# A recommendation tower on one core: layer 2 turned round, layer 3 as a row sum on VectorE, and layer 1 of two sample tiles joined

## What is computed

```python
e = stack([tbl_f[ids[:, f]] for f in range(27)], axis=1)      # 512 x 27 x 128
z = einsum('bnd,bmd->bnm', e, e)[:, c, r]                      # 351 pairs per sample
h = concatenate([z, dense_ctx], axis=1)                        # 512 x 367
h = maximum(h @ W_top1 + b_top1, 0.0)                          # 512 x 512
h = maximum(h @ W_top2 + b_top2, 0.0)                          # 512 x 256
y = h @ W_top3                                                 # 512 x 1
```

## Time and profile before

| | us |
|---|---|
| median of 3 runs | 124.17 |
| lowest, highest run | 122.57, 124.36 |
| span of the profiled execution | 123.6 |
| TensorE matmul busy in it | 106.3 (86%) |
| VectorE busy | 70.0 (57%) |
| ScalarE busy | 67.2 (54%) |

### The profile page before, as it was taken

The page is one execution under the profiler, slowest core; times in us unless marked ns, Lnnn a source line. Parts: engine busy times, 40 slices in busy tenths (PEclk is TensorE's granted clock), DMA queues, the critical chain, the costliest instruction groups (busy, mean ns, idle before and its releaser), DMA issues.

```text
span 123.6 us, 3473 instructions
## 1 busy us (share of the span) xinstructions
PE 106.3 (86%) x1496; PEld 86.1 (70%) x1496; DVE 70.0 (57%) x98; ACT 67.2 (54%) x112; POOL 68.1 (55%) x71
## 2 busy tenths in 40 slices
PE   6998799899999899999329993789458999997992
PEld 6534487687887687788219883669448999797891
DVE  6799999999999999999900050015001060103401
ACT  4596929899999999995200052025301144531442
POOL 3777888888888888887744166416560665000000
PEclk9999999999999999999985599558975699999999
DMA  3896366966984574711210101110200011000000
GB/s 79 262 237 190 101 204 146 293 198 155 302 235 111 172 229 108 205 48 42 54 52 17 31 29 42 27 48 21 66 24 27 21 48 41 23 5 5 5 0 1
DMA packets 5305, 12.06 MB, mean 98 GB/s; under 512 B 1765, under 2 KB 2277, under 8 KB 5290
## 3 DMA queue, kind: packets, MB, share of 16 engines
q1 hardware_dynamic: 3282, 7.75, 22.0%
q0 software_dynamic: 1984, 4.07, 12.8%
q10 hardware_dynamic: 24, 0.02, 0.1%
HBM read 11.83 MB, written 0.00 MB: 96 GB/s over the span
## 4 chain that ended last, share of the span: by engine, by line
PE 68%; DVE 16%; issue 13%; ACT 1%; DVEq 0%
PE ring L512 21%; PE gram_ps L539 12%; DVE marks L651 10%; PE gram_ps L512 8%; PE ring L592 5%; PE ids_ps L574 4%; PE ring L523 4%; DVE low L628 3%; PE ids_ps L567 2%; PE ids_ps L523 2%; PE ring L574 2%; PE ring L602 2%; PE ids_ps L592 1%; DVE pick L610 1%; PE ids_ps L553 1%
## 5 line engine op out<-in xcount | busy, mean ns | idle before, releaser
L422 POOL DMA_INDIRECT rows<-tbl,ids_sb x62 | 67.1, 1082 | 36.3 <-issue 15.9
L651 DVE TENSOR_TENSOR marks<-ids_ps,row_no 125x1024 fp32r<-125x1024 f32 (+2 forms) x39 | 43.5, 1148 | 0.0
L512 PE MATMUL ring<-marks,high 125*128 125x512 f32 (+1 forms) x64 | 26.6, 416 | 1.7 <-issue 1.6
L539 PE MATMUL gram_ps<-rowsT 128*27 128x27 f32 x1024 | 15.8, 206 | 11.4 <-issue 11.2
L512 PE MATMUL ring<-marks,low 125*128 125x512 f32 (+1 forms) x64 | 25.2, 394 | 0.0
L539 PEld LDWEIGHTS gram_ps<-rowsT 128*27 128x27 f32 x1024 | 13.3, 118 | 14.7 <-issue 14.0
L512 PEld LDWEIGHTS ring<-marks,high 125*128 125x128 f32 x64 | 12.8, 200 | 7.1 <-issue 4.6
L724 ACT ACTIVATE away<-ids_ps,row_no 125x512 f32<-125x512 f32 (+1 forms) x22 | 14.0, 715 | 4.7 <-PE ids_ps L466 4.1
L628 DVE TENSOR_TENSOR low<-raw,high 125x512 fp32r<-125x512 f32 (+1 forms) x23 | 16.2, 705 | 0.0
L672 DVE STREAM_TRANSPOSE gram<-gram_ps 128x416 f32<-128x416 f32 (+1 forms) x8 | 4.6, 612 | 18.1 <-PE gram_ps L539 18.1
L512 PEld LDWEIGHTS ring<-marks,low 125*128 125x128 f32 x64 | 12.9, 202 | 1.6
(11 more groups left out here) (61 smaller groups left out, 116.5 us busy)
## 6 DMA issues: line engine op xcount, KB each, us to landing
raw<-tbl SPq DMA_DIRECT2D x9, 448.0 KB
raw<-tbl SPq DMA_DIRECT2D x2, 560.0 KB
rows<-tbl,ids_sb POOLq DMA_INDIRECT x62
w_sb<-w SPq DMA_DIRECT2D x2, 256.0 KB
w_sb<-w SPq DMA_DIRECT2D x1, 512.0 KB
raw<-tbl SPq DMA_DIRECT2D x9, 52.0 KB
raw<-tbl SPq DMA_DIRECT2D x2, 224.0 KB
w_sb<-w SPq DMA_DIRECT2D x1, 192.0 KB
```

What stands on the lines that cost most here:

```text
L422: nc.gpsimd.indirect_dma_start(out=rows[0:n, i % ROW_BUFS, s, :], out_offset=None, in_=tables[PLACES[s]], in_offset=bass.IndirectOffsetOnA ...
L512: last = nc.tensor.matmul(bank[:, 0:n], part[:, i % SPLIT_BUFS, c * D:(c + 1) * D], mark_of(unit, c), start=c == 0 and part is high, stop= ...
L539: last = nc.tensor.matmul(gram_ps[s * STRIP:s * STRIP + F, g, 0:F], places, places, start=True, stop=True)
L651: nc.vector.tensor_tensor(marks_of(unit)[:, c0 - c1:, :], index.to_broadcast([TP, c1 - c0, n]), which.to_broadcast([TP, c1 - c0, n]), ALU. ...
```

## The change

- Layer 2 takes h1T as the stationary operand and w2 as the moving one, so that samples come out on the partitions and the 256 outputs in the columns: four matmuls of 256 columns a tile in place of eight of 128, one bank in place of two. VectorE adds b2 (line 700 after) and, in a second instruction, clips, multiplies by w3 and sums along the row into one column of y_cols (line 703). b2 and w3 come as rows repeated on 128 partitions, one more load of 256 KB (last_rows). ScalarE has no part in layer 2 any more.
- Layer 3's matmuls go. After the last tile one matmul of y_cols with the identity turns the four columns into four rows ("out 0", line 608), ScalarE copies them, SyncE writes them.
- Layer 1 runs three times, for tile 0, for tiles 1 and 2 together with 256 samples moving, and for tile 3 (LAYER1).
- ORDER changes from the step after pairs 1 2 on, and gather 60 waits for pairs 2 0 ("paired 7").

```diff
 BANK = 512
-M1, M2 = H1 // P, H2 // P
+M1 = H1 // P
 TILES = [(b, P) for b in range(0, B, P)]
+LAYER1 = [(0, 1), (1, 2), (3, 1)]
+L1_MOST = max(n for _, n in LAYER1) * P
+def layer1_of(i):
+    return [k for k, (i0, n) in enumerate(LAYER1) if i0 <= i < i0 + n][0]
...
 l1 0 2, l1 0 3, l1 0 4, gram 2 0, gram 2 1, gram 2 2, pairs 1 0, turn 3 0, pairs 1 1, pairs 1 2
-l2 0 0, l2 0 1, gram 2 3, l3 0, l1 1 0, turn 3 1, l1 1 1, l1 1 2, l1 1 3, l1 1 4, l2 1 0, pairs 2 0
-l2 1 1, pairs 2 1, pairs 2 2, turn 3 2, l3 1, l1 2 0, turn 3 3, l1 2 1, gram 3 0, gram 3 1, l1 2 2
-l1 2 3, l1 2 4, gram 3 2, gram 3 3, l2 2 0, l2 2 1, pairs 3 0, pairs 3 1, l3 2, pairs 3 2, l1 3 0
-l1 3 1, l1 3 2, l1 3 3, l1 3 4, l2 3 0, l2 3 1, l3 3
+gram 2 3, l2 0 0, l2 0 1, turn 3 1, pairs 2 0, pairs 2 1, pairs 2 2, l1 1 0, turn 3 2, l1 1 1
+l1 1 2, l1 1 3, l1 1 4, l2 1 0, turn 3 3, l2 1 1, gram 3 0, gram 3 1, gram 3 2, gram 3 3
+l2 2 0, l2 2 1, pairs 3 0, pairs 3 1, pairs 3 2, l1 2 0, l1 2 1, l1 2 2, l1 2 3, l1 2 4
+l2 3 0, l2 3 1, out 0
 """
...
 44 gram_part 3, 46 marks_used 50, 48 gram_part 5, 50 products 2, 52 l1_done 1, 54 gram_part 7, 56 paired 6
-58 products 3, 60 l1_done 7
+58 products 3, 60 paired 7
 """
...
         return [(kind, i)] if part[0] == 0 else []
-    if kind in ("l1", "l2"):
-        return [(kind, i, m) for m in range(M1 if kind == "l1" else M2)] if part[0] == 0 else []
+    if kind == "l1":
+        return [(kind, i, m) for m in range(M1)] if part[0] == 0 else []
+    if kind == "l2":
+        return [(kind, i)] if part[0] == 0 else []
     return [] if kind == "gram" else [step]
...
                     sp.dma_start(w2_sb[:, :, :], w2.rearrange("(m p) n -> p m n", p=P)).then_inc(w2_in, 16)
-            sp.wait_ge(y_ready, len(TILES))
-            sp.dma_start(out, y_sb[:, :]).then_inc(out_done, 16)
+                if k == 5 + BLOCKS:
+                    sp.dma_start(last_sb[:, :, :], last_rows).then_inc(last_in, 16)
+            sp.wait_ge(y_ready, 1)
+            sp.dma_start(out.rearrange("o (t p) -> (o t) p", p=P), y_sb[:, :]).then_inc(out_done, 16)
             sp.wait_ge(out_done, 16)
...
                 elif kind == "l1":
-                    b0, n = TILES[i]
+                    i0, tiles = LAYER1[i]
+                    b0, n = TILES[i0][0], tiles * P
                     part = step[2]
...
                         banks = [use_ring(use) for use in takes(step)]
-                        wait_z(i, 0)
+                        wait_z(i0 + tiles - 1, 0)
                         for m in range(M1):
...
                             if m == 0:
-                                wait_z(i, c)
+                                wait_z(i0 + tiles - 1, c)
                             last = nc.tensor.matmul(ring_bank(("l1", i, m))[:, 0:n],
...
                         pe.wait_ge(w2_in, 16)
-                    if half == 0:
-                        banks = [use_ring(use) for use in takes(step)]
-                    else:
-                        banks = [ring_bank(("l2", i, m)) for m in range(M2)]
+                    bank = use_ring(("l2", i)) if half == 0 else ring_bank(("l2", i))
+                    k = layer1_of(i)
+                    at = (i - LAYER1[k][0]) * P
                     for c in range(half * M1 // 2, (half + 1) * M1 // 2):
-                        pe.wait_ge(h1_ready, M1 * i + c + 1)
-                        for m in range(M2):
-                            last = nc.tensor.matmul(banks[m][:, 0:n], w2_sb[:, c, m * P:(m + 1) * P],
-                                                    h1T[:, c, 0:n], start=c == 0, stop=c == M1 - 1)
-                            if c == M1 - 1:
-                                last.then_inc(l2_done, 1)
-                elif kind == "l3":
-                    n = TILES[i][1]
+                        pe.wait_ge(h1_ready, M1 * k + c + 1)
+                        last = nc.tensor.matmul(bank[0:n, 0:H2], h1T[:, c, at:at + n], w2_sb[:, c, :],
+                                                start=c == 0, stop=c == M1 - 1)
+                    if half == 1:
+                        last.then_inc(l2_done, 1)
+                elif kind == "out":
                     bank = use_ring(step)
-                    for c in range(M2):
-                        wait_h2(i, c)
-                        last = nc.tensor.matmul(bank[0:1, 0:n], w3_sb[:, c:c + 1], h2T[:, c, 0:n],
-                                                start=c == 0, stop=c == M2 - 1)
-                    last.then_inc(l3_done, 1)
+                    pe.wait_ge(y_col_ready, len(TILES))
+                    nc.tensor.matmul(bank[0:len(TILES), 0:P], y_cols[:, :], ident[:, :],
+                                     start=True, stop=True).then_inc(y_turned, 1)
...
                     if i == 0:
-                        dve.wait_ge(small_in, 16)
-                    dve.wait_ge(l2_done, M2 * i + 2)
-                    nc.vector.tensor_scalar(h2T[:, 1, 0:n], ring_bank(("l2", i, 1))[:, 0:n], b2_sb[:, 1:2], 0.0,
-                                            ALU.add, ALU.max).then_inc(h2_ready_too, 1)
+                        dve.wait_ge(last_in, 16)
+                    else:
+                        dve.wait_ge(y_col_ready, i)
+                    dve.wait_ge(l2_done, i + 1)
+                    nc.vector.tensor_tensor(h2[0:n, :], ring_bank(("l2", i))[0:n, 0:H2], b2_sb[0:n, :],
+                                            ALU.add).then_inc(h2_ready, 1)
+                    dve.wait_ge(h2_ready, i + 1)
+                    nc.vector.scalar_tensor_tensor(h2[0:n, :], h2[0:n, :], 0.0, w3_sb[0:n, :], ALU.max, ALU.mult,
+                                                   accum_out=y_cols[0:n, i:i + 1]).then_inc(y_col_ready, 1)
         @block.scalar
         def _(act):
             nc.scalar.dma_start(fids[:, :], found_ids).then_inc(fids_in, 16)
             act.wait_ge(ident_ready, 1)
-            nc.scalar.activation(h2T[:, 0, 0:1], ident[:, 0:1], ACT.Abs)
+            nc.scalar.activation(h1T[:, 0, 0:1], ident[:, 0:1], ACT.Abs)
...
                 elif kind == "l1" and step[2] > 0:
-                    n = TILES[i][1]
+                    n = LAYER1[i][1] * P
                     m = step[2] - 1
                     if i == 0 and m == 0:
-                        act.wait_ge(small_in, 16)
+                        act.wait_ge(b1_in, 16)
                     act.wait_ge(l1_done, M1 * i + m + 1)
                     nc.scalar.activation(h1T[:, m, 0:n], ring_bank(("l1", i, m))[:, 0:n], ACT.Relu,
                                          bias=b1_sb[:, m:m + 1]).then_inc(h1_ready, 1)
-                elif kind == "l2" and step[2] == 1:
-                    n = TILES[i][1]
-                    act.wait_ge(l2_done, M2 * i + 1)
-                    nc.scalar.activation(h2T[:, 0, 0:n], ring_bank(("l2", i, 0))[:, 0:n], ACT.Relu,
-                                         bias=b2_sb[:, 0:1]).then_inc(h2_ready, 1)
-                elif kind == "l3":
-                    b0, n = TILES[i]
-                    act.wait_ge(l3_done, i + 1)
-                    nc.scalar.copy(y_sb[0:1, b0:b0 + n], ring_bank(step)[0:1, 0:n]).then_inc(y_ready, 1)
+                elif kind == "out":
+                    act.wait_ge(y_turned, 1)
+                    nc.scalar.copy(y_sb[:, :], ring_bank(step)[0:len(TILES), 0:P]).then_inc(y_ready, 1)
...
-        "small": np.concatenate([x.reshape(-1, P).T for x in (b1, b2, w3)], axis=1),
+        "b1": np.ascontiguousarray(b1.reshape(-1, P).T),
+        "last_rows": np.tile(np.concatenate([b2.reshape(1, H2), w3.reshape(1, H2)], axis=1), (P, 1)).reshape(P, 2, H2),
         "denseT": np.ascontiguousarray(np.asarray(inputs["dense_ctx"]).T),
```

More of the change, by code:

```diff
@@ L231, in marks_order, with build @@
     return before
-def build(nc, ids, found_ids, tables, w1, w2, small, denseT, out):
+def build(nc, ids, found_ids, tables, w1, w2, b1, last_rows, denseT, out):
     ctx = ExitStack()
@@ L267, in build @@
         w2_sb = sb("w2_sb", [P, M1, H2])
[L268 to L272, removed]
+        b1_sb = sb("b1_sb", [P, M1])
+        last_sb = sb("last_sb", [P, 2, H2])
+        b2_sb, w3_sb = last_sb[:, 0, :], last_sb[:, 1, :]
+        h1T = sb("h1T", [P, M1, L1_MOST])
+        h2 = sb("h2", [P, H2])
+        y_cols = sb("y_cols", [P, len(TILES)])
+        y_sb = sb("y_sb", [len(TILES), P])
         ident = sb("ident", [P, P])
@@ L286, in build @@
         w2_in = sem("w2_in")
-        small_in = sem("small_in")
+        b1_in = sem("b1_in")
+        last_in = sem("last_in")
         dense_in = sem("dense_in")
@@ L322, in build @@
         h2_ready = sem("h2_ready")
-        h2_ready_too = sem("h2_ready_too")
-        l3_done = sem("l3_done")
+        y_col_ready = sem("y_col_ready")
+        y_turned = sem("y_turned")
         y_ready = sem("y_ready")
@@ L375, in _ @@
                 if k == 1:
-                    sp.dma_start(small_sb[:, :], small).then_inc(small_in, 16)
+                    sp.dma_start(b1_sb[:, :], b1).then_inc(b1_in, 16)
                 if k == 4:
```

(8 more changed lines are left out.)

## The result

| | before | changed |
|---|---|---|
| median, 6 runs each, us | 124.17 | 129.87 |
| lowest, highest | 122.57, 124.44 | 127.93, 131.44 |
| ratio, 95% interval | | 1.045 (1.037 to 1.053) |
| span of the profiled execution | 123.6 | 129.6 |
| gram products (L539, now L548), idle put down to issue | 11.2 | 14.0 |

The change makes the kernel 4.5% slower, where 0.3% faster was forecast; the time lies far outside the range. The execution profiled after the change was the slowest of its six (131.44), with more time at the low clock than the others, so its span is not set against the forecast, and ratios leave such executions out.

What follows compares the result with a forecast made beforehand. TensorE's time was taken to bound the late part: 22.45 us against 23.37 gains 0.92, the tail loses 0.52, so −0.40 on a 123.6 us span; with 0.6 carried over to the median, 123.8 us, range 122.1 to 125.7.

Steps and rivals of the forecast that it cites:

- Step 1: gram 2 3, moved ahead of layer 2 of tile 0, at the low clock: 0.90 us.
- Step 7: gram 3 in one run: 1.23 + 2.08 us, with one pause of 0.66 us kept.
- (c): gram 2 3 starves beside gathers issued at 95.96 and 97.21 us: +1.7, 125.5 us; chance 0.09.
- (b): gram 3, one run of 256 records, gets one or two more 0.7 us pauses: 124.5 to 125.2 us; chance 0.13.
- step 2: Layer 2 of tile 0, 8 records of 256 columns, partly before the clock rises: 2.65 us.
- step 3: turn 3 1 and three pairs, 7 records, after layer 2 of tile 0: 0.77 us.
- Steps 4 and 8: TensorE waits 0.80 us before joint layer 1; layer 2 of tile 2 and pairs 3 take 3.35, including 1.24 wait.
- rival (d): The clock stays at 1.2 GHz past 98.2 us, costing 2.8 us of work: 126.6 us; chance 0.06.
- The rival order: A z copy not behind VectorE's sum would take away both TensorE waits and 1.7 us; no chance given.
- The wide records: Layer 1 and layer 2 records with 256 columns moving: 0.2225 us each at full clock; joining layer 1 saves only starts.
- The tail: From the start of the last layer 2 to the copy of y: 3.69 us against 3.17, 0.52 lost.
- The load of last_rows: 256 KB on SyncE's queue ahead of three table loads: costed at 0, 0.3 to 1 us if a table comes late.

Runs made afterwards that it cites:

- e3: Kernel before with only the last part of gram 2 moved ahead of layer 2 of tile 0; median 128.68 us, ratio 1.036.
- e6: Changed kernel with gathers from the 56th on waiting for the end of gram 2, not pairs 1 2; four runs, median 127.07 us.
- e2: Changed kernel with 16 one-column matmuls (64 instructions) put at the start of TensorE's program; one run, 128.89 us.
- e5: Changed kernel with gram 3 in two halves again, layer 1 and layer 2 work between them; median 128.20 us, ratio 1.037.
- e7: Changed kernel with the edits of e5 and e6 together; median 125.28 us, ratio 1.003 to the kernel before.
- e8: e7 with VectorE's row sum of tiles 0 and 2 behind the z copies; median 124.58 us, ratio 1.001.
- e9: e4 with VectorE's two tile 2 instructions behind z copies and layer 1's first step taking banks one at a time; median 122.42 us, ratio 0.984.
- e4: Changed kernel's layers 2 and 3, but layer 1 per tile and TensorE's order as before; median 125.61 us, ratio 1.004.
- e1: Changed kernel with layer 2 of tile 0 ahead of the last part of gram 2 again; median 128.98 us, ratio 1.032.
- e10: e9 with tile 2's pairs and turn 3 2 moved ahead, layer 2 of tile 1 partly between gram 3's halves; median 123.07 us, ratio 0.987.
- e12: e10 plus gather 54 waiting for pairs 1 0 instead of the first part of gram 2; median 123.06 us, ratio 0.978.

## Why the prediction was wrong

The step that failed is the pricing of gram products in a new place, steps 1 and 7. Their work was priced rightly and their pauses were not, though both rivals that describe them stood in the text, (c) with 9% and (b) with 13%. They came together. In the profiled execution, 1.6 us above the median, the stretch from gram 2 3 to the last layer 2 took 29.09 us (95.26 to 124.35) for the 22.45 forecast. Of these 6.6 us, steps 1 and 7 hold 4.2; steps 2, 3 and 8, which ran wholly or in part at the low clock, hold 3.0; the wait of step 4 was 0.6 shorter.

- **Step 1, gram 2 3 at 0.90 us: 3.3 us.** Rival (c) is what happened. The text let the part just escape, on the thought that all 128 instructions are taken in before the gather starts. In the trace 50 records went through, 14 were left (41 had run on in the earlier trace rows), and three pauses followed. e3 shows the move alone costs 3.6%, e6 that the gathers are the cause. That price holds more than the 2.4 us of step 1: the low clock lasted to 102.4 us in e3's profile and to 104.2 after the change, and made layer 2 and what follows it slow (after the change 3.57 us for the 2.65 of step 2, 1.7 for the 0.77 of step 3). That is rival (d), which the text took for an independent case; it came with (c) in these two, though not in e2.
- **Step 7, one long pause kept at its old length: 2.62 us for 0.66.** Here rival (b) is right in place and wrong in kind. There weren't one or two more pauses but the same one, longer. It ends 1.45 to 1.56 us after a packet of 16 KB has landed, and from instruction 2560 to the pause's end it took 3.26 us before and 3.65 after (2.9 to 3.7 in the nine kernels with this pause). Before, the first half of gram 3 and 1.5 us of layer 1 filled most of that time; the joined run went through 194 instructions in under a microsecond and waited for the rest. The Trainium skill, Runtime: NRT & Kernel Launch, section Instruction fetch mechanics, has blocks of 256 instructions in 16 KB, which the packet's size and e5's pause, 256 instructions ahead, bear out. It calls the crossing of a block mostly hidden, which it isn't for gram products: 2.62 us stood open.
- **Steps 4 and 8, the waits for VectorE.** Right. 0.80 and 1.24 were forecast; without a low clock in the way they were 0.74 and 1.11 (e7), released by the z copy. In the changed kernel's own profile, where slow records covered them in part, they were 0.19 and 0.82. The rival order, named at the end of the prediction as worth 1.7 us, took 0.8 off the two waits in e8 and gave 2% in e9 against e4, more than the one wait of 1.1 us that it mends; what else helped e9 was not taken apart.
- **The wide records (steps 2, 5, 6).** 0.215 us in e4's layer 2 for the 0.2225 taken. Joining layer 1 brings nothing, as said.
- **The tail.** 3.69 forecast; in the changed kernel 124.35 to 128.07, 3.72.
- **The load of last_rows.** Costed at nothing, and right: ScalarE's casts waited 0.3 us for tables in all, as before.

So the steps other than 1 and 7 were priced about right, as e7 (1.003) shows: once both pauses are gone, the forecast's 0.997 is nearly met, and the stretch of the sum took 22.67 us (95.83 to 118.50) for 22.45. In part that is luck: e7's gram 3 has no pause at all where 0.84 us was kept for one, and its late rows cost 0.85 us that were in no step.

## What to carry to other kernels

An order of steps has prices that no step has alone: a dense run of tiny matmuls broke where gathers were issued beside it and waited where a block of instructions came late, so keep transfers that GpSimd issues out of it and put slow work between blocks of 256 instructions. A pause at a fixed place in an engine's instruction stream can be found by putting harmless instructions in front: if it moves by their number, it belongs to the stream and not to the work. And a cheaper tail of products (layer 3) is worth what the engine behind it leaves: move that engine's work off the path first, as e9 does, and then the saving shows.

## What the runs showed of the hardware

- While gathers were issued, gram products ran in bursts of 1 to 6 records, mostly 5 or 6, mostly 0.71 to 0.76 us from one to the next, in every kernel and wherever the gathers lay; without gathers 128 records took 1.23 us.
- The pause at instruction 2753 or 2754 was 2.62, 2.33, 2.31 and 1.91 us in a run of 256 records (changed, e2, e6, e1), 0.66 to 0.33 us where gram 3 was in halves with 1.5 us between, and none with 2.4 us or more (e5, e7, e8, e10, e12); e5 had one of 0.45 us at instruction 2497.
- The clock stood at 1.2 GHz from 90.6 to 104.2 us in the changed kernel's profile and rose at 97.4 in e2's, the same program but for 64 instructions. How much of the 4.5% is the clock's, and how much the pauses' own, is therefore not settled. One comparison bounds it: e2's run, with a mean granted clock of 0.946, took 128.89 us, and two of the kernel before beside it, at 0.945, took 124.91 and 125.22, so in this one run some 3.7 to 4.0 us stood at an equal clock. That the clock falls after pauses is only seen, since no run held one fixed.
